# First attention of a two-layer block: the gain of the keys' normalisation moved out of V into the evictions of keys and of AV, the pooled part added by the DVE

## What is computed

```python
h = layernorm(x) * (1 + ca) + sa
q = rotary(h @ w_q) * scale; kv = rotary(h @ w_kv)      # 16 heads of 64
lkv = ln(windows of kv, previous window and own) * ln_local_g + ln_local_b
pkv = softmax(segments of 16 rows of kv @ w_proj)
gkv = ln(sum over the segment of kv * pkv) * ln_global_g + ln_global_b
sim = concat([q @ gkv.T masked, q @ lkv.T masked]); attn = softmax(sim)
out = attn @ concat([gkv, lkv])          # the normalised keys are the values too
x = x + ga * (out @ w_out + b_out)
```

## Time and profile before

| | us |
|---|---|
| median of 3 runs | 1521.95 (1512.76 to 1534.51) |
| the profiled execution, its own time | 1513.62 |
| its span, first to last instruction | 1511.8 |
| PE, DVE, ACT, POOL busy | 1200.5, 931.4, 822.3, 725.5 |
| mean granted TensorE clock, of full speed | 0.896 |

### The profile page before, as it was taken

How to read it: one execution, slowest core, us unless ns; L and a number is a source line. 1 busy time by engine, 2 the same in 40 slices (tenths; PEclk the granted TensorE clock), 3 DMA queues, 4 the chain that set the end, 5 groups by cost and what they waited for, 6 DMA issues and landing times. The chain is left out here.

```text
span 1511.8 us, 30131 instructions
## 1 busy us (share of the span) xinstructions
PE 1200.5 (79%) x9299; PEld 928.5 (61%) x9299; DVE 931.4 (62%) x2122; ACT 822.3 (54%) x2181; POOL 725.5 (48%) x750
## 2 busy tenths in 40 slices
PE   3368988989889993898899899889937887888436
PEld 1245665656656662898899889889913444444336
DVE  4687787787876533744744664764434677776633
ACT  1256777767677771676676666666612443344101
POOL 2646748567485312565566556556653323211223
PEclk8589999989998995999999999999966999899558
DMA  7500000000000003303003000000063445331145
GB/s 221 174 2 3 1 10 3 8 10 0 9 2 8 10 8 127 124 11 125 8 11 120 16 9 10 12 12 7 10 174 81 84 87 104 58 48 21 23 121 152
DMA packets 152775, 76.43 MB, mean 51 GB/s; under 512 B 99992, under 2 KB 143384, under 8 KB 152408
## 3 DMA queue, kind: packets, MB, share of 16 engines
q1 hardware_dynamic: 144696, 66.42, 16.8%
q0 software_dynamic: 3072, 6.31, 1.3%
q10 hardware_dynamic: 4896, 2.36, 0.5%
HBM read 54.77 MB, written 19.76 MB: 49 GB/s over the span
## 5 line engine op out<-in xcount | busy, mean ns | idle before, releaser
L1477 POOL TENSOR_TENSOR hl<-hid,hh 128x256 fp32r<-128x256 f32 x396 | 294.0, 744 | 218.8 <-ACT hh L1454 215.1
L1520 DVE SCALAR_TENSOR_TENSOR hid<-GU,gub,sg 128x256 f32<-128x256 f32 x396 | 190.5, 482 | 194.7 <-ACT sg L1448 123.5
L1348 PE MATMUL GU<-xh,wh 128*128 128x256 f32 x792 | 233.3, 295 | 39.4 <-DVE wl L1496 30.3
L1448 ACT ACTIVATE sg<-GU,gub 128x256 f32<-128x256 f32 x396 | 188.1, 475 | 123.6 <-PE GU L1350 121.7
L1349 PE MATMUL GU<-xl,wh 128*128 128x256 f32 x792 | 225.3, 284 | 0.0
L1350 PE MATMUL GU<-xh,wl 128*128 128x256 f32 x792 | 225.1, 284 | 0.0
L1348 PEld LDWEIGHTS GU<-xh,wh 128*128 128x128 f32 x792 | 152.1, 192 | 49.0 <-issue 27.3
L1454 ACT CAST hh<-hid 128x256 fp32r<-128x256 f32 x396 | 158.2, 399 | 25.8 <-DVE hid L1520 25.3
L1349 PEld LDWEIGHTS GU<-xl,wh 128*128 128x128 f32 x792 | 152.5, 193 | 0.0
L1350 PEld LDWEIGHTS GU<-xh,wl 128*128 128x128 f32 x792 | 152.2, 192 | 0.0
L648 ACT ACTIVATE prob<-prob,rZ 128x272 f32<-128x272 f32 (+1 forms) x256 | 98.9, 462 | 60.6 <-DVE rZ L1021 55.2
(11 more groups left out here) (312 smaller groups left out, 2842.6 us busy)
## 6 DMA issues: line engine op xcount, KB each, us to landing
raw<-in_expert_w SPq DMA_DIRECT2D x4, 2688.0 KB, 12.0
late<-in_w SPq DMA_DIRECT2D x20, 256.0 KB, 6.1
raw<-in_expert_w SPq DMA_DIRECT2D x4, 1152.0 KB, 6.1
list<-zero SPq DMA_DIRECT2D x4, 1024.0 KB, 8.6
modb<-mod_d SPq DMA_DIRECT2D x9, 384.0 KB, 4.3
early<-rel_d SPq DMA_DIRECT2D x1, 3072.0 KB, 13.1
qkv_d<-qkv SPq DMA_DIRECT2D x48, 64.0 KB
early<-in_w SPq DMA_DIRECT2D x12, 256.0 KB, 4.2
```

Of the source, the lines that this page charges most:

```text
L1348: pe.matmul(out, lhs[0], rhs[0], start=start, stop=False, skip_group_check=True)
L1448: act.activation(sg[:, c % BUFS], GU[c % BUFS][:, 0:TT], ACT.Silu, bias=gub[:, GATE, e * CH0 + c:e * CH0 + c + 1]).then_inc(silu, 1)
L1477: pool.tensor_tensor(hl[:, b], hid[:, b], hh[:, b].bitcast(F32), ALU.subtract).then_inc(hid_lo, 1)
L1520: dve.scalar_tensor_tensor(out=hid[:, c % BUFS], in0=GU[c % BUFS][:, TT:2 * TT], scalar=gub[:, UP, e * CH0 + c:e * CH0 + c + 1], in1=sg[:, ...
```

## The change

V is no longer multiplied by ln_local_g: `scale_keys` is gone from the POOL. Instead a column gainT, ln_local_g twice down the partitions, is made once by two more matmuls and a copy. The keys' eviction gets it as a scale (in transposed keys a partition is a dimension of the head). In AV the part of V goes into columns 0 to 255 of bank O and the pooled part into columns 256 to 511; the ACT writes the first, times gainT, into a new tile attV, and the DVE adds the second and writes attT (`attention_out`). The ACT's eviction counts av_out, the DVE's addition counts aT_out. The addition of pair n - 3 stands in the DVE's step n, behind the rotation. The wait for a full "out" bank before attT is overwritten moves from the ACT to the DVE. kv_norm counts 2 a batch, and the DMA of rel_d uses the semaphore rel_in.

```diff
--- before.py
+++ after.py
@@ -245,6 +245,7 @@
         gk = sb("gk", [P, 4, DH0])
         gs = sb("gs", [P, 4, DH0])
         shiftT = sb("shiftT", [P, P])
+        gainT = sb("gainT", [P, 1])
         gv = sb("gv", [32, 2, HP, P])
         kT = sb("kT", [P, 2, HP, KW])
         qt = sb("qt", [P, 2, NT])
@@ -255,6 +256,7 @@
         prob = sb("prob", [P, 2, 2 * SCOLS])
         pT = sb("pT", [P, 2, 2, 512])
         attT = sb("attT", [P, HP, NT])
+        attV = sb("attV", [P, NT])
         res = sb("res", [P, TILES, D])
         x1 = keep["x1"]
         bn2 = sb("bn2", [P, TILES, 6])
@@ -293,7 +295,7 @@
         cast = sem("cast")
         
         silu_c = sem("silu_c"); modT_mm = sem("modT_mm"); modT_out = sem("modT_out"); mod_mm = sem("mod_mm"); mod_step = sem("mod_step"); mod_out = sem("mod_out")
-        rel_in = sem("rel_in"); rel_mm = sem("rel_mm"); rel_out = sem("rel_out"); rel_d = sem("rel_d")
+        rel_in = sem("rel_in"); rel_mm = sem("rel_mm"); rel_out = sem("rel_out");
         filled = sem("filled"); taken = sem("taken")
         x_in = sem("x_in"); modb_in = (sem("modb_in0"), sem("modb_in1")); wq_in = sem("wq_in")
         ln_step = sem("ln_step")
@@ -308,7 +310,7 @@
         hq = sem("hq"); q_mm = sem("q_mm"); q_rot = sem("q_rot"); q_sum = sem("q_sum")
         s_mm = sem("s_mm"); s_max = sem("s_max"); s_exp = sem("s_exp")
         pT_mm = sem("pT_mm"); pT_out = sem("pT_out")
-        z_recip = sem("z_recip"); p_norm = sem("p_norm"); o_mm = sem("o_mm"); aT_out = sem("aT_out")
+        z_recip = sem("z_recip"); p_norm = sem("p_norm"); o_mm = sem("o_mm"); aT_out = sem("aT_out"); av_out = sem("av_out")
         r_step = sem("r_step"); ln2_rstd = sem("ln2_rstd"); n2_done = sem("n2_done"); h2_done = sem("h2_done")
         t_step = sem("t_step"); t_exp = sem("t_exp"); slot_out = sem("slot_out"); kv_rstd = sem("kv_rstd"); g_rstd = sem("g_rstd")
         scat = sem("scat"); count_mm = sem("count_mm"); count_out = sem("count_out")
@@ -351,8 +353,8 @@
             sp.dma_start(modb[:, 1:], mod_d[0, 1:].partition_broadcast(P)).then_inc(modb_in[1], 16)
 
             sp.wait_ge(rel_out, 1)
-            sp.dma_start(io["rel_d"], relt[:]).then_inc(rel_d, 16)
-            sp.wait_ge(rel_d, 16)
+            sp.dma_start(io["rel_d"], relt[:]).then_inc(rel_in, 16)
+            sp.wait_ge(rel_in, 48)
 
             sp.wait_ge(set_up, ZERO_SET)
             for e in range(E0):
@@ -401,8 +403,9 @@
             mm.then_inc(modT_mm, 1)
             pe.wait_ge(w_in, 16 * n_w)
             pe.wait_ge(modT_out, 1)
-            for e in range(2):
-                mm = pe.matmul(O[e * DH0:(e + 1) * DH0, NT:NT + P], lng[:, 1, :], ident, start=True, stop=True)
+            for k in range(2):
+                for e in range(2):
+                    mm = pe.matmul(O[e * DH0:(e + 1) * DH0, NT - k * P:NT - k * P + P], lng[:, 1 - k, :], ident, start=True, stop=True)
             mm.then_inc(modT_mm, 1)
 
             def shift_out():
@@ -464,7 +467,7 @@
 
             def kT_mm(slot, b, bp, c):
                 if c == 0:
-                    pe.wait_ge(kv_norm, 4 * (b + 1))
+                    pe.wait_ge(kv_norm, 2 * (b + 1))
                 bank, a = use(f"kT{c}", slot)
                 for u in range(2):
                     for k in range(TILES):
@@ -523,12 +526,12 @@
                     pe.wait_ge(cast, 3)
                 else:
                     pe.wait_ge(aT_out, n)
-                pe.matmul(O[:, 0:NT], gv[:, bp, hp, :], pT[0:32, pb, :, 3 * P:4 * P], start=True, stop=False, skip_group_check=True)
+                pe.matmul(O[:, NT:], gv[:, bp, hp, :], pT[0:32, pb, :, 3 * P:4 * P], start=True, stop=True, skip_group_check=True)
                 for kt, first, keys in ((0, 0, 0), (1, P, 2 * P)):
                     for e in range(2):
                         head = (2 * hp + e) * DH0
                         mm = pe.matmul(O[e * DH0:(e + 1) * DH0, first:NT], V[:, bp, kt, head:head + DH0],
-                                       pT[:, pb, e, keys:keys + NT - first], start=False, stop=(kt == 1), skip_group_check=True)
+                                       pT[:, pb, e, keys:keys + NT - first], start=(kt == 0), stop=(kt == 1), skip_group_check=True)
                 mm.then_inc(o_mm, 1)
 
             def out_mm(slot, b):
@@ -629,6 +632,7 @@
             act.wait_ge(modT_mm, 1)
             act.copy(modT[:].rearrange("p m b -> p (m b)"), O[:, 0:5 * NB]).then_inc(modT_out, 1)
             act.wait_ge(modT_mm, 2)
+            act.copy(gainT[:], O[:, P:P + 1])
             act.copy(shiftT[:], O[:, NT:NT + P]).then_inc(modT_out, 1)
 
             def exponentials(n, hp):
@@ -659,7 +663,7 @@
                     if c == 0 and not known_zero(b - 1):
                         act.wait_ge(s_mm, HP * (b - 1))
                     act.activation(kT[:, np_, 2 * c:2 * c + 2, NSEG:KEYS[1]], a[:].rearrange("p (u k) -> p u k", u=2),
-                                   ACT.Identity, bias=shiftT[:, 0:1]).then_inc(bank.drained, 1)
+                                   ACT.Identity, bias=shiftT[:, 0:1], scale=gainT[:, 0:1]).then_inc(bank.drained, 1)
 
                 for hp in range(HP):
                     n = slot * HP + hp
@@ -696,9 +700,9 @@
                     if (late if hp < 2 else heads):
                         m = n - 2
                         act.wait_ge(o_mm, m + 1)
-                        if late and hp == 2:
-                            bank0.wait_full(act, "out", slot)
-                        act.copy(attT[:, (hp - 2) % HP, :], O[:, 0:NT]).then_inc(aT_out, 1)
+                        if not known_zero(m):
+                            act.wait_ge(aT_out, m)
+                        act.activation(attV[:], O[:, 0:NT], ACT.Copy, scale=gainT[:, 0:1]).then_inc(av_out, 1)
                     if last:
                         m, pb = n - 1, (hp - 1) % 2
                         act.wait_ge(pT_mm, m + 1)
@@ -831,7 +835,7 @@
                 if known_zero(b):
                     dve.wait_ge(mod_out, 16)
                 else:
-                    dve.wait_ge(kv_norm, 4 * b)
+                    dve.wait_ge(kv_norm, 2 * b)
                 dve.scalar_tensor_tensor(out=heads_of(kvc[:, t, :]), in0=mean[:, t, :, None].broadcast_to([P, H0, DH0]),
                                          scalar=-1.0 / DH0, in1=heads_of(kvr[:, t, :]), op0=ALU.mult,
                                          op1=ALU.add).then_inc(kv_c, 1)
@@ -1026,6 +1030,8 @@
                         i.then_inc(s_max, 1)
                     if (heads if hp < HP - 1 else early):
                         rotate_queries(n + 1, (hp + 1) % 2)
+                    if (late if hp < 3 else heads):
+                        attention_out(slot, n - 3, hp)
                     if isinstance(slot, int) and slot == 0 and hp == 0:
                         dve.wait_ge(w_in, 16 * n_w)
                         dve.wait_ge(modT_mm, 3)
@@ -1073,6 +1079,12 @@
                     if late and hp == 7:
                         list_places(slot, l)
 
+            def attention_out(slot, m, hp):
+                dve.wait_ge(av_out, m + 1)
+                if hp == 3 and not (isinstance(slot, int) and slot == 0):
+                    bank0.wait_full(dve, "out", slot)
+                dve.tensor_tensor(attT[:, (hp - 3) % HP, :], attV[:], O[:, NT:], ALU.add).then_inc(aT_out, 1)
+
             def rotate_queries(n, buf):
 
                 dve.wait_ge(q_mm, n + 1)
@@ -1146,12 +1158,6 @@
                 for t in range(TILES):
                     pool.tensor_tensor(heads_of(V[:, bp, t, :]), heads_of(kvc[:, t, :]),
                                        krs[:, t, :, None].broadcast_to([P, H0, DH0]), ALU.mult).then_inc(kv_norm, 1)
-
-            def scale_keys(b, bp):
-                for t in range(TILES):
-                    pool.wait_ge(kv_norm, 4 * b + 1 + t)
-                    pool.tensor_tensor(heads_of(V[:, bp, t, :]), heads_of(V[:, bp, t, :]), per_head(lng[:, 0, :]),
-                                       ALU.mult).then_inc(kv_norm, 1)
 
             def weigh(slot, b):
                 bank1.wait_emptied(pool, "pkT", slot)
@@ -1203,8 +1209,6 @@
                         if not known_zero(b):
                             weigh(slot, b)
                         normalise(b, np_)
-                    if early and hp == 4:
-                        scale_keys(b, np_)
                     if early and hp == 5 and known_zero(b):
                         normalise_pooled(slot, b)
                     if norm and hp == 5:
```

## The result

| | before | after |
|---|---|---|
| median, us | 1527.41 (5 runs: the three known before, two more beside the changed kernel) | 1596.16 (5 runs, 1583.99 to 1598.87) |
| profiled execution, us | 1513.62 | 1583.99 |
| its span | 1511.8 | 1582.2 |
| PE, DVE, ACT, POOL busy | 1200.5, 931.4, 822.3, 725.5 | 1216.3, 945.1, 837.1, 679.8 |

The ratio is 1.0469, 95% interval 1.0424 to 1.0514: slower; it compares the fast runs and comes out only without the run of 1534.51 us of the kernel before, while the two medians as they stand give 1.0450. The range of the prediction (1533 to 1598) holds the median of 1596.16, but only just, and its point of 1567 is 29 us under it. Forecast were 45 us by the medians and 50 by the spans; measured are 69 by the medians and 70.4 by the spans of the two profiled executions.

What follows compares the result with a forecast made beforehand. The PE's instruction order bounds early head pairs, the DVE later ones, never the POOL. Terms 33 + 7 + 12.7 + 0.5 + 2.5 - 5.5 = +50 us on 1513.6 gave 1564, put at 1567; range 1533 to 1598.

Steps and rivals of the forecast that it cites:

- batch 6: Batch without a later batch's normalisation: 5.25 us for pairs 1 to 3, 1.2 for pairs 5 to 7, 0.5 for pair 0.
- last batch, 7 steps: Last batch, without that DVE work: all eight steps exposed, 12.7 us, of which 11 lie between the scores.
- all between the scores: First to last scores: 33 us for batches 1 to 5, 7 for batch 6, 2.5 for batch 0, 11 for the last.
- The loop through scores, maxima, rotation, addition and AV: Exposed head pairs: AV waits for the same step's DVE addition, +1.75 us, a step costing 6.9 us instead of 5.16.
- their cover: ACT: 8 us of longer evictions hidden by 120 us of idle time, priced at nothing; without it 1 us a batch.
- The prologue: Before the first scores the POOL is the chain; dropping its multiplication moves everything forward, -5.5 us once, first scores near 76.
- the first rival: PE clock falls once more per batch, some 7 us at half speed: +24 us, hence 1590; chance 0.12.
- the gaps near pair 7: Argument against a worse clock: present PE gaps preceding the fall at 204 us get smaller because AV moves into them.
- the sign named for it: Would show the worse clock: a granted clock clearly under 0.93 between the first scores and the last.
- the half of a batch in which the DVE is full: Pairs 6, 7 and 0: DVE additions count whole, 3 x 0.42 = +1.3 us per batch for batches 0 to 5.
- relief of 0.7 from blocked DVE instructions: DVE rotation sum L1085 waits less for the POOL once its multiplication goes: 0 to 1.6 us per batch, 0.7 taken.
- the tail: Behind the last scores: one addition between the last eviction and the output projection, +0.5 us.

Runs made afterwards that it cites:

- e6_fill_all: The changed kernel with useless bf16 matmuls filling all PE gaps ahead of AV, in every head pair; 1564.89 us, ratio to the kernel before 1.0299.
- e10_fill_three: The kernel before with useless matmuls in pair 7 and, in pair 0, both ahead of and behind its transposes; 1519.15 us, ratio 0.9981.
- e1_add_first: The changed kernel with the DVE's addition moved ahead of the maxima, nothing left out; 1517.58 us, ratio to the kernel before 0.9989.
- e2_wait_alone: The kernel before with only one more wait: AV waits for the same step's rotation; 1553.85 us, ratio 1.0220.
- e5_no_add: The kernel before with gain as eviction scales and pooled values divided by the gain, so no DVE addition; 1511.7 us, ratio 0.9938.
- e3_pool_kept: The changed kernel with the POOL's two multiplications of V put back, now by ones; 1595.23 us, ratio to the kernel before 1.0496.

## Why the prediction was right and where it was wrong

With the clock at 0.98 on both sides (17.1 and 21.6 us at 1.2 GHz), e6_fill_all less e10_fill_three is what the new order costs. From scores to scores, in us, mean of batches 1 to 5, then whole batches (the last from its first scores to its last):

| | before | filled | after | filled | filled less filled | forecast |
|---|---|---|---|---|---|---|
| pair 0 | 8.47 | 7.94 | 9.92 | 8.05 | +0.1 | +0.4 |
| pair 1 | 5.22 | 5.04 | 7.11 | 6.71 | +1.7 | +1.75 |
| pair 2 | 8.71 | 8.70 | 10.60 | 10.60 | +1.9 | +1.75 |
| pair 3 | 4.86 | 4.87 | 6.53 | 6.53 | +1.7 | +1.75 |
| pair 4 | 9.51 | 9.51 | 10.37 | 10.05 | +0.5 | +0.4 |
| pair 5 | 7.75 | 7.76 | 8.57 | 8.24 | +0.5 | -0.3 |
| pairs 6 and 7 | 17.76 | 17.74 | 16.55 | 16.81 | -0.9 | +0.8 |
| a batch of 1 to 5 | 62.3 | 61.6 | 69.7 | 67.0 | +5.4 | +6.6 |
| batch 0 | 60.2 | 60.2 | 62.4 | 63.0 | +2.8 | +2.5 |
| batch 6 | 56.1 | 57.5 | 66.0 | 60.8 | +3.3 | +7 |
| last batch, 7 steps | 40.0 | 40.5 | 56.5 | 50.2 | +9.7 | +11 |
| all between the scores | 467.7 | 465.9 | 533.2 | 508.9 | +43.0 | +53.5 |

"Filled" is e10_fill_three in its first column and e6_fill_all in its second. The pause of 3 us lies in pair 0 of batch 4 in the unfilled kernels and mostly in pair 7 of batch 3 in the filled ones, so up to 0.6 us of these two rows is only its place.

**Right: the mechanism and its price.** The loop through scores, maxima, rotation, addition and AV costs 1.7 to 1.9 us in pairs 1 to 3, where 1.75 was worked out from the timeline of before. Pairs 1 to 3 together: forecast 5.25, measured 5.2. In the last batch it is 1.3 to 1.9 us in each of pairs 1 to 6 and nearly nothing in pair 0. Undoing the order alone undoes the loss (e1_add_first), making the wait alone makes nearly half of it (e2_wait_alone).

**Right: the single durations.** The addition took 0.411 us (0.387 to 0.421) where L920 gave 0.424. The ACT's evictions with a scale took 0.475 us, 0.10 more than without (0.08 taken), and the keys' 0.789, 0.085 more (0.09 taken); e1_add_first has them too and loses nothing, so their cover held but for what its 0.5% over e5_no_add may hold. The group in the changed kernel:

```profile
L705 ACT ACTIVATE attV<-O,gainT 128x256 f32<-128x256 f32 x64 | 30.4, 475 | 94.9 <-PE O L533 92.7 <-issue 2.2
```

By the Trainium skill ("ScalarE: Activation LUTs", section "What ACT_TABLE_LOAD costs") a pointer operand adds about 93 ns; the trace agrees, with 99 ns for the first (475 less 376) and 85 for the second (789 less 704). The prologue gave 4.3 where 5.5 was taken: first scores at 77.4, not 76.

**Wrong: the clock, priced at nothing in the sum.** This is the step that failed. 65.5 less 43.0, so 22.5 us between the scores, are the lower clock. The sum had no term for it; it stood as the first rival, "3 us x 8 = +24", at a chance of 0.12. That the size came out to 2 us is luck: the rival took one more fall of some 7 us in each of eight batches, 56 us at 1.2 GHz at 0.43 us each, and measured are 28 us more at 1.2 GHz that cost 22.5. It was argued against because the gaps near pair 7 would get smaller. But the slow stretches there stayed: pairs 6, 7 and 0 together took 26.5 us in the changed kernel and 24.9 filled; and falls in pair 1 and in the last batch came on top. The argument looked at the one gap that existed, not at the many that the change makes. Nor would the sign named for it, a granted clock clearly under 0.93, have told: between the scores it is 0.92 against 0.93. The PE's busy time, said to stay unchanged, tells more: between the scores it went from 413.4 to 425.3 us with the same matmuls. What tells best is the time at 1.2 GHz, 89.7 against 61.5 us, and still more where it lies. Before it lay beside a full DVE and 44 us of it cost 1.8; in the changed kernel the PE and the DVE take turns, so a slow PE step lengthens the loop: 68 us less at 1.2 GHz gave 24.3, about 0.36 us each. Pair 1 of batch 2, fallen, took 9.16 us; pair 1 of batch 1, not fallen, 6.62.

**Wrong: the half of a batch in which the DVE is full, 1.2 us a batch too dear, and batch 6, 3.7.** The additions were counted whole, 1.3 a batch, against a relief of 0.7 from blocked DVE instructions. Between the scores the DVE is busy 352.27 us before and 364.16 after, 11.9 more, though the additions are some 24.7 (60 at 0.411): the relief is 12.8, or 1.6 a batch. Its largest part is the rotation sum, first before, then after:

```profile
L1085 DVE TENSOR_TENSOR qr<-qt 128x256 f32<-128x256 f32 x64 | 42.3, 661 | 2.2
```

```profile
L1097 DVE TENSOR_TENSOR qr<-qt 128x256 f32<-128x256 f32 x64 | 32.8, 512 | 2.2
```

The reason given, the POOL's removed multiplication, isn't borne out: with the multiplication kept (e3_pool_kept) the DVE is busy 365.20, so nearly the same 12 us are saved. What is left is that the two queues stand otherwise against one another; no run tests this by itself. That the DVE, which waits longer for scores in pairs 1 to 3, comes to pairs 6 and 7 with less left over is likely and not shown either.

**Wrong, small: the tail and the rest.** The tail took 4.9 us more in this execution, 1.4 with the gaps filled, forecast was 0.5 and one step of 1.75. The rest gave 4.4, forecast was nothing; they go with its clock (188 us at 1.2 GHz there, before 177), and that the change plays no part in them is not shown.

**The sum again, against the spans.** All in us, measured and in brackets forecast. Prologue -4.3 (forecast -5.5), order 43.0 (53.5), clock 22.5 (0), tail 4.9 (2.3 with the eighth step), rest 4.4 (0): 70.5. These are single executions. The ratios, each against the kernel before of its own session, give 0.0170 less 0.0019 for the clock, 23 us, the same; but e6_fill_all less e10_fill_three is 0.0318, 48 us, with intervals of some 6 and 4 us, where the two spans without their rest give only 38.9 (-4.3, 43.0 and 0.2). So the clock's part stands on both, while the order costs between 43 and some 52 us, and how much too dear it was priced is uncertain by as much. By the spans there were two errors of opposite sign, of 10 and of 22, so that the median still fell within the range is in part luck; the larger error was the term that had been given a chance but no place in the sum.

**What stays open.** Why the clock falls in pair 1 of some batches and not of others with the same instructions: batches 2 and 5 of the changed kernel differ in pair 1 by 2.4 us and in no other step by more than 0.5, and no row read here tells them apart beforehand. Nor is a batch the same from kernel to kernel: batch 5 and the last batch, whose steps e3_pool_kept leaves as they are, have 6.8 and 13.7 us at 1.2 GHz in the changed kernel and 13.7 and 0.0 in that one. Useless matmuls have a price of their own, too: in the kernel before they lengthened batch 6 by 1.4 us, so 43.0 and 22.5 are each uncertain by a few us for this reason alone.

## What to carry to other kernels

A short instruction that moves to another engine takes on everything that stands ahead of it in that queue: read which engine waits for its result, and put it ahead of whatever needs that engine's next result. With the 0.41 us of this one ahead of the maxima the whole change cost nothing, between maxima and rotation 0.8%, and behind both 4.7%. Where a change opens gaps on the PE in every step, price the clock as a term of the sum and ask whether another engine covers the slow stretches; a mean granted clock of two digits hardly moves (0.93 to 0.92 here); the time at the lower level tells more. Where a factor can be divided out of the smaller operand, as here of the pooled keys (which asks that no gain is zero), the partial sums stay in PSUM and no addition is needed. Before a difference of a few us is read from two profiled executions, set their times at the lower level beside each other.

## What the runs showed of the hardware that was not expected

- A PE that waits 1.65 us in each step of 6.5 us and works in between ran at 2.4 GHz in most steps and fell to 1.2 GHz in some: 89.7 of 533 us at the lower level, 71.9 with the waits of pairs 1 to 3 and of the last batch filled, 21.6 with all filled. The same steps fall in one execution and not in another: the last batch had 13.7 us at 1.2 GHz in the changed kernel and none in e3_pool_kept, unfilled.
- Filling one gap can move the fall of the clock to the next gap instead of removing it: with pair 7 filled in the kernel before, 71.6 us were spent at 1.2 GHz instead of 61.5, and they lay where they cost 3.8 us in each of four batches; with pairs 7 and 0 filled, in three places, 17.1 us.
- A DVE instruction of two SBUF inputs, 0.42 us at best, took 0.66 in the mean before, 0.51 after and 0.53 after with the POOL's multiplication kept; what else could lengthen it than the way in which the queues of POOL and DVE fall together no run shows. By the Trainium skill ("SBUF — State Buffer", section "SBUF: two separate sides") DVE and GpSimd share a pair of ports as an exclusive lock; the trace agrees so far as the addition L1086, with one input in PSUM, was never longer than 0.421 us in 64 times.
- The identical instructions behind the attention took 921 to 936 us in the twelve profiled executions, with a granted clock of 0.904 in the shortest and 0.885 in the two longest. The same holds for whole runs: the 56 of the kernel before measured beside the experiments took 1512 to 1536 us with granted clocks of 0.897 to 0.875, the slower the lower, 0.27 us for each us at 1.2 GHz by a straight line. One profiled execution therefore doesn't tell effects of a few us.
